# The scan's 3x3 convolution: the lower row's three taps on TensorE's 64-row tiles, the other six on VectorE alone

## The reference, cut to what matters

```python
xz = conv1x1(xin, in_proj_w)
xc, z = (xz[:, :Cm], xz[:, Cm:])                       # Cm = 64
z = jax.nn.silu(z)
xc = jax.lax.conv_general_dilated(xc, conv_w, (1, 1), 'SAME', feature_group_count=Cm, ...) + conv_b
xc = jax.nn.silu(xc)                                   # a 3x3 depthwise convolution of 64 channels
xh = xc.reshape(Bb, Cm, L)
xw = xc.transpose(0, 1, 3, 2).reshape(Bb, Cm, L)       # the same, column by column
```

## Time and profile before

| | |
|---|---|
| time, median of 3 runs | 3703.48 us (3699.1 to 3704.27) |
| the profiled execution: span | 3694.3 us |
| PE busy | 2966.0 us, 80% |
| PE weight loads busy | 1600.3 us, 43% |
| DVE busy | 2489.1 us, 67% |
| ACT busy | 2368.6 us, 64% |
| POOL busy | 1081.3 us, 29% |
| mean granted clock of TensorE | 0.93 |

### The profile page before, as it was taken

How to read it: one execution, slowest core, us unless ns; L and a number is a source line. 1 busy time by engine, 2 the same in 40 slices (tenths; PEclk the granted TensorE clock), 3 DMA queues, 4 the chain that set the end, 5 groups by cost and what they waited for, 6 DMA issues and landing times.

```text
span 3694.3 us, 53955 instructions
## 1 busy us (share of the span) xinstructions
PE 2966.0 (80%) x17500; PEld 1600.3 (43%) x17500; DVE 2489.1 (67%) x2565; ACT 2368.6 (64%) x2681; POOL 1081.3 (29%) x612
## 2 busy tenths in 40 slices
PE   3688876969978877787997887776998788768699
PEld 2344335435534434434553443443555344344355
DVE  5787656866478656687466964768636786577771
ACT  2887545468688745447778864543868877454484
POOL 0235103632034500463103530146210453025430
PEclk9899998979989999898998999888999999989899
DMA  2001473600200157440020034653002005555101
GB/s 67 17 1 39 119 203 104 164 9 0 69 27 1 44 133 215 112 125 9 0 90 5 0 91 120 198 142 79 9 9 86 0 0 141 130 173 146 40 0 52
DMA packets 137191, 274.31 MB, mean 74 GB/s; under 512 B 17139, under 2 KB 93622, under 8 KB 137014
## 3 DMA queue, kind: packets, MB, share of 16 engines
q1 hardware_dynamic: 137014, 272.01, 26.5%
HBM read 194.07 MB, written 77.88 MB: 74 GB/s over the span
## 4 chain that ended last, share of the span: by engine, by line
PE 50%; DVE 24%; issue 11%; ACT 9%; DMA 3%; POOL 1%; DVEq 1%; SPq 1%; ACTq 0%; POOLq 0%
PE psum L1074 31%; PE psum L1094 5%; PE psum L1327 5%; DVE work L1501 5%; DVE work L1473 3%; PE psum L1125 3%; DVE region L1602 3%; DVE psum L1492 2%; DVE region L277 2%; DVE work L1486 2%; DMA work<-scratch_dwc 2%; PE psum L1285 2%; PE psum L1286 1%; DVE region L1546 1%; DVE region L1670 1%
## 5 line engine op out<-in xcount | busy, mean ns | idle before, releaser
L1556 DVE SCALAR_TENSOR_TENSOR work<-region,cols,work 128x768 f32<-128x768 f32 x288 | 397.9, 1382 | 16.6 <-DVE work L1556 8.1
L735 POOL TENSOR_TENSOR region<-region 128x768 f32<-128x768 f32 x96 | 205.8, 2147 | 376.2 <-ACT region L919 370.5
L1074 PE MATMUL psum<-region,m_cen 128*128 128x384 f32 (+1 forms) x384 | 163.9, 553 | 171.0 <-DVE region L1670 64.0
L1074 PE MATMUL psum<-region,m_fc 128*128 128x384 f32 (+1 forms) x768 | 282.8, 491 | 11.0 <-ACT work L1026 11.0
L1327 PE MATMUL psum<-work,m_fc 128*128 128x384 f32 x768 | 282.7, 492 | 1.2 <-DVE region L1674 0.9
L699 POOL TENSOR_TENSOR work<-work 128x768 f32<-128x768 f32 x48 | 109.3, 2280 | 440.8 <-ACT work L840 370.9
L1074 PE MATMUL psum<-work,m_avg 128*128 128x384 f32 x576 | 225.6, 516 | 15.1 <-ACT work L881 7.2
L711 POOL TENSOR_TENSOR work<-work,region 128x768 f32<-128x768 f32 x96 | 174.5, 1818 | 214.1 <-DVE work L1486 214.1
L277 DVE SCALAR_TENSOR_TENSOR region<-region,cols 128x768 f32<-128x768 f32 x192 | 223.8, 1165 | 19.9 <-POOL region L735 9.9
L1026 ACT ACTIVATE work<-psum,cols 128x768 f32<-128x768 f32 x192 | 173.1, 901 | 91.1 <-PE psum L1074 89.2
L1473 DVE SCALAR_TENSOR_TENSOR work<-region,cols,work 128x768 f32<-128x768 f32 x144 | 192.6, 1358 | 52.4 <-POOL work L699 34.2
(11 more groups left out here) (234 smaller groups left out, 7539.0 us busy)
## 6 DMA issues: line engine op xcount, KB each, us to landing
work<-scratch_cpe SPq DMA_DIRECT2D x192, 196.0 KB, 4.1
work<-scratch_dwc SPq DMA_DIRECT2D x192, 196.0 KB, 4.1
work<-scratch_lepe SPq DMA_DIRECT2D x192, 196.0 KB, 3.9
region<-in_tab_ch SPq DMA_DIRECT2D x48, 768.0 KB, 5.3
region<-in_x SPq DMA_DIRECT2D x48, 384.0 KB, 3.3
region<-in_tab_tok SPq DMA_DIRECT2D x48, 384.0 KB, 3.2
out<-work SPq DMA_DIRECT2D x48, 384.0 KB, 2.4
scratch_cpe<-region SPq DMA_DIRECT2D x44, 392.0 KB, 4.4
```

What stands on the lines that cost most here:

```text
L735: g.tensor_tensor(chain_tile(conv, n, p), chain_tile(conv, n - 1, p), chain_tile(conv, n, p), ALU.add).then_inc(tap_done[n], 1)
L1074: last = pe.matmul(psum[:, bank + s, 0:HC], weights[:, :], moving(s), start=(n == 0), stop=(n == len(terms) - 1))
L1556: v.scalar_tensor_tensor(out=by_row(tile(acc + p)), in0=prow(k, b, *TAPS[n]), scalar=tap_weight(conv, TAPS[n]), in1=by_row(tile(acc + p)), ...
```

## The change: what it does

The taps of the row below go to TensorE, and ScalarE and GpSimd leave the convolution. `lower[n]` is `same_half` with its rows scaled by the tap of the row below at column offset `n - 1`; a late load puts these taps into the upper partitions of `cols` too. For each block TensorE does six matmuls on 64 rows of the array: for each of three column offsets, one on partitions 0 to 63 for the first four rows of the block (bank `2 * p`), one on partitions 64 to 127 for the last four (bank `2 * p + 1`). It does them before it waits for VectorE, and then two matmuls with `same_half` for the other six taps. VectorE does those six as three instructions: one product of a tensor and a column, and two that multiply and add.

`overlapped` gets a list of runs that are never folded into a loop; on TensorE the convolution's run is one, so that its twelve blocks are written out. SyncE waits for all loads to land before it issues the late loads. Two unused diagonal matrices and `dwl1` are no longer made; three matrices `lower` are.

```diff
-                if not all(1 <= b <= count - 2 for b in bs):
+                if n in static or not all(1 <= b <= count - 2 for b in bs):
                     return None
...
+        below = slice(at["l1taps"] + 3, at["l1taps"] + 6)
+        late_loads = [(cols[CM:P, below], t["cols"][0:CM, below])]
...
             sp.wait_ge(setup_vec, 1)
+            sp.wait_ge(setup_loaded, 16 * len(loads))
             for dst, src in late_loads:
...
-                    g.tensor_tensor(tile(4 + p), tile(p), tile(2 + p), ALU.add).then_inc(b_taps[0], 1)
...
-                    a.wait_ge(b_taps[0], done(i, b - 2))
-                    for n, signal_of in enumerate((b_first, b_second)):
-                        a.activation(by_row(tile(2 * n + p)), prow(3, b, *scan_tap(n)), ACT.Copy, scale=col("l1taps", n))\
-                            .then_inc(signal_of, 1)
-                return [(0, first_terms), (3, silu_u)]
+                return [(3, silu_u)]
...
                     pe.wait_ge(b_act, done(i, b - 2))
-                    pe.wait_ge(b_taps[3], done(i, b))
-                    product(2 * p, [(dwl1, image_rows(3, b, *scan_tap(5))), (same_half, static(tile(6 + p)))])\
-                        .then_inc(b_mm, 1)
+                    pe.wait_ge(a_act, done(i, following(b)))
+                    for n in range(3):
+                        for s in range(2):
+                            half = slice(CM * s, CM * s + CM)
+                            rows = padded(3)[half, ds(ROWS * b + (2 + (HALF - 1) * s), HALF), n:n + S]
+                            pe.matmul(psum[:, 2 * p + s, 0:HC], lower[n][half, :], rows, start=(n == 0), stop=False)
+                    pe.wait_ge(b_taps[2], done(i, b))
+                    for s in range(2):
+                        last = pe.matmul(psum[:, 2 * p + s, 0:HC], same_half[:, :], static(tile(6 + p))(s), start=False,
+                                         stop=True)
+                    last.then_inc(b_mm, 1)
...
+            v.wait_ge(late_loaded, 16 * len(late_loads))
+            for n in range(3):
+                v.tensor_scalar(lower[n][:, :], same_half[:, :], col("l1taps", 3 + n), None, ALU.mult)
...
+                def first_tap(b, p):
+                    if is_first(b):
+                        for q in range(2):
+                            v.wait_ge(h_store[q], i * (8 * NB) + 16)
+                    v.wait_ge(a_act, done(i, following(b)))
+                    v.tensor_scalar(by_row(tile(p)), prow(3, b, -1, -1), col("l1taps", 0), None, ALU.mult)\
+                        .then_inc(b_taps[0], 1)
+                def second_tap(b, p):
+                    v.wait_ge(b_taps[0], done(i, b))
+                    v.scalar_tensor_tensor(out=by_row(tile(4 + p)), in0=prow(3, b, -1, 0), scalar=col("l1taps", 1),
+                                           in1=by_row(tile(p)), op0=ALU.mult, op1=ALU.add).then_inc(b_taps[1], 1)
+                def third_tap(b, p):
+                    v.wait_ge(b_taps[1], done(i, b))
+                    v.wait_ge(b_mm, done(i, b - 2))
+                    v.scalar_tensor_tensor(out=by_row(tile(6 + p)), in0=prow(3, b, -1, 1), scalar=col("l1taps", 2),
+                                           in1=by_row(tile(4 + p)), op0=ALU.mult, op1=ALU.add).then_inc(b_taps[2], 1)
```

More of the change, by code:

```diff
@@ L98, in chained, with overlapped @@
             step(t)
-def overlapped(eng, count, runs):
+def overlapped(eng, count, runs, static=()):
     def blocks(t):
@@ L227, in build @@
         same_half = mat("same_half")
-        dwl1 = mat("dwl1")
+        lower = [mat(f"lower_{n}") for n in range(3)]
         w_dt = [mat(f"w_dt{n}") for n in range(2)]
@@ L234, in build @@
         convs = ("cpe1", "dwc", "lepe", "cpe2")
-        diag = {c: [mat(f"{c}_{n}") for n in range(9 - CHAIN)] for c in convs if c == "cpe2"}
         shifted = {c: mat(c + "_shifted", 3 * P) for c in convs[:3]}
@@ L306, in build @@
         a_act = signal("a_act", "a")
-        b_first = signal("b_first", "a")
-        b_second = signal("b_second", "a")
-        b_taps = [signal(f"b_taps{n}", "g" if n == 1 else "v") for n in range(1, 5)]
+        b_taps = [signal(f"b_taps{n}", "v") for n in range(3)]
         b_mm = signal("b_mm", "p")
@@ L460, in build @@
                               t["cols"].rearrange("(j c) n -> c j n", j=4)[:, :, c0:c0 + 3]))
-        late_loads = []
+        below = slice(at["l1taps"] + 3, at["l1taps"] + 6)
+        late_loads = [(cols[CM:P, below], t["cols"][0:CM, below])]
         for k in range(4):
@@ L471, in build @@
                                        t["x_proj"][2 * sweep + half, RANK + what:RANK + what + 1, :]))
-        def scan_tap(n):
-            return (-1, n - 1) if n < 3 else (1, n - 4)
         def by_row(ap):
@@ L693, in middle @@
                 clear_frame(padded(3), last=2)
[L695 to L698, removed]
-                    g.tensor_tensor(tile(4 + p), tile(p), tile(2 + p), ALU.add).then_inc(b_taps[0], 1)
-                pipelined(g, NB, [(1, first_sum)])
                 all_done(g, i - 1, h_mm)
@@ L1335, in middle @@
                        (3, g_variance), (4, up(3)), (4, down(2)), (2, g_centre)]
-                overlapped(pe, NB, [(0, mlp)] + following_runs)
-            overlapped(pe, NB, [(0, [(3, xz(0)), (0, l0(0))]), (NB, conv_run(0))])
+                overlapped(pe, NB, [(0, mlp)] + following_runs, static=(2,))
+            overlapped(pe, NB, [(0, [(3, xz(0)), (0, l0(0))]), (NB, conv_run(0))], static=(1,))
             with pe.Fori(0, B - 1, 1) as i:
@@ L1387, in _ @@
             link(v.reduce_sum(col("Dsum"), cols[:, at["l1_D"]:at["l1_D"] + 4], mybir.AxisListType.X))
[L1388 to L1392, removed]
             link(v.tensor_tensor(shift_mask[:, :], ident[:, 0:32], ident[:, 32:64], ALU.add))
@@ L1401, in _ @@
                                         None, ALU.mult)
-            v.tensor_scalar(dwl1[:, :], same_half[:, :], col("l1taps", 5), None, ALU.mult)
             v.tensor_scalar(w_in[:, :], raw_in, col("n1_g"), None, ALU.mult)
@@ L1465, in conv_run @@
             def conv_run(i):
[L1466 to L1478, removed]
+                def first_tap(b, p):
[14 more added lines that the diff above has]
+                                           in1=by_row(tile(4 + p)), op0=ALU.mult, op1=ALU.add).then_inc(b_taps[2], 1)
+                return [(2, first_tap), (2, second_tap), (2, third_tap)]
             def middle(i, following_runs):
```

## The result

The changed kernel takes 3672.22 us in the median (3667.39 to 3676.65), against 3703.88 for the kernel before on the same chip: a ratio of 0.9917, 95% interval 0.9901 to 0.9932, 31.7 us faster. Two later comparisons gave 0.9938 (0.9926 to 0.995) and 0.9907 (0.9886 to 0.9928), 21.5 and 33.6 us faster. The forecast was 3667 us. The profiled span fell from 3694.3 to 3665.6 us, by 28.7.

The account below looks back on a forecast made before the run. VectorE and GpSimd taking turns, 4.73 us a block, were taken as the bound; TensorE's 3.48 makes a stage 46.1 us, saving 36.5 together: 3694.3 - 36.5 = 3657.8, with 9.2 around it 3667 us, range 3650 to 3676.

Parts of the forecast that it names:

- VectorE and GpSimd as the bound before: Convolution stage before the change: VectorE's taps and GpSimd's sum take turns and bound a block at 4.73 us.
- VectorE's steps: VectorE per block after: a product of 0.72, two multiply-and-adds of 1.02, gaps of 0.45; 3.2 us, at most 3.9.
- TensorE's lower row, six waves: TensorE per block: twelve instructions on two 64x128 tiles, row halves side by side, in six waves, 2.10 us.
- TensorE's `same_half`, 1.38: TensorE per block: the product with `same_half` as four instructions of 0.32 plus 0.09 for the change of tiles, 1.38 us.
- The rule of the Trainium skill: TensorE: changing tiling mode drains it, two changes per block; priced from the trace at 0.09 and 0.16, within the 3.48.
- The stage: Convolution stage per image: 12 x 3.48 + 1.7 for the clock + 2.6 tail = 46.1 us, together saving 36.5.
- Clock: Start of the stage: one dip of 3.4 us at half speed, 1.7 lost; the later dips dropped.
- Head, set-up, written-out code: Stage head: nothing; set-up: nothing, at worst 2 us once; TensorE's written-out blocks: nothing taken, bound 12 us.
- the 9.2 us "around" the profiled span: Whole run: 9.2 us added to the forecast span of 3657.8, giving 3667 us.
- halves one after another: Rival, TensorE's lower row: row halves don't run side by side on 64x128 tiles, 14 us longer per image, 3759; 7%.
- A drain for a matmul's whole 0.48: Rival, TensorE: each change of tiles empties the array for 0.48, 4.2 a block, no change, 3701; 4%.
- Clock at the low level, VectorE or code in the way: Two rivals: clock stays at 0.50, 3827, 2%; VectorE or code fetch holds TensorE, half the gain lost, 3685, 12%.

Follow-up runs that it names:

- experiments 2 to 4: The changed kernel with ScalarE's two products and GpSimd's sum kept: 3694.11 us; then the sum on VectorE: 3693.04 us; or one product on VectorE, GpSimd summing: 3678.73 us.
- experiment 6: The changed kernel with a fourth VectorE instruction per block, a second copy of the first product into an unused tile: 3674.22 us, 0.9937 to the kernel before.
- experiment 1: The changed kernel with the lower row's six matmuls on all 128 rows, zero weights for the upper partitions: 3754.04 us, 1.014 to the kernel before.
- experiment 7: The changed kernel with the lower rows of two blocks, then both products, in eight PSUM banks: 3663.99 us, 0.989 to the kernel before.
- experiment 4: The changed kernel with GpSimd's sum kept, one of its two products on ScalarE, the other on VectorE: 3678.73 us, 0.9929 to the kernel before.

## Why the prediction was right, point by point

- **VectorE and GpSimd as the bound before**: right for the first bound, incomplete for the second. The working showed ScalarE busy for 44.7 of 52.5 us and passed over it; experiments 2 to 4 show that it would have been the next bound, 4.30 per block. The limits stand close together: 4.73 for VectorE with GpSimd, 4.30 for ScalarE, 3.62 for TensorE. The change takes work from ScalarE too, so the number did not suffer. ScalarE's figure stood in its timeline before the change: from the two products of one block to those of the next are 1062.84 - 1058.52 = 4.32 us, without idle time.

```profile
1058.52 1.76 ACT L840 ACTIVATE work<-region,cols 128x768 f32 x2
1060.31 0.90 ACT L829 ACTIVATE region<-psum,cols 64x768 f32 x1
1061.21 1.60 ACT L831 ACTIVATE region<-psum,cols 64x768 f32 x1
1062.84 1.76 ACT L840 ACTIVATE work<-region,cols 128x768 f32 x2
```

- **VectorE's steps**: the new product takes 0.61 (estimate 0.72), a block without waiting is 2.7 (3.62 less 0.91), below the 3.2. That TensorE doesn't wait for it is shown by experiment 6.
- **TensorE's lower row, six waves**: right in kind, 2.14 for 2.10. Pairs start 5 to 10 ns apart, and experiment 1 shows what the overlap is worth.
- **TensorE's `same_half`, 1.38**: this is the term that was mis-sized, with 1.49 measured. It was taken from the product at 650.32, which follows matmuls of its own height. The product that comes out of small tiles stands two rows below it: 1.56 from 653.80, against 1.45. Those 0.11 us are the second half of the price of a change, and they were in the rows. With the 0.04 of the lower row a block is 3.625: 48 x 0.145 = 7.0 us too little.
- **The rule of the Trainium skill ("TensorEngine Tiling (Array Packing)", Key Properties)**, that a change of the mode drains TensorE: the trace agrees in that a change costs 0.20 us, and experiment 7 confirms the price by taking half of the changes away. An emptied array the trace doesn't show: the first 128-row matmul starts at 1052.876, and the last 64-row one, from 1052.465, is given 0.481 us, so 0.07 us longer (ends of matmuls are modelled). No figure but the measured one entered.
- **The stage**: 12 x 3.625 + 1.7 + 2.6 = 47.8, which images 1 and 2 have. Images 0 and 3 meet the low clock for longer at the start (first block 6.2 us, 146.31 to 152.53, and 5.9, 2833.28 to 2839.17, not 5.3 as from 1041.84 to 1047.12). Together the stages save 28.1 instead of 36.5; of the 8.4 missing, 7.0 come from the block and 1.5 from these heads.
- **Clock**: right. One low stretch at the head and none later: behind the first block all of TensorE's blocks take 3.62 us, in all images of the three profiles. The 64-row tiles don't lower the clock.
- **Head, set-up, written-out code**: nothing was taken for them, and nothing is seen. The written-out blocks have no run of their own; TensorE shows no pause inside the stage. TensorE's set-up moved from 27.11 to 29.34 (29.2 was said), and L0 began at 56.5 us instead of 57.1. That image 0's stage began 4.0 us earlier (146.31, before 150.28) belongs to that one execution: in the two later profiles of the changed kernel it began at 150.0 and 149.9. Some 3.4 us the other way lie in the rest of the program (28.1 + 4.0 - 3.4 = 28.7, the fall of the span).
- **From span to median**: the 9.2 us "around" the profiled span were mostly not around it. A run's time is 1.8 to 2.0 us above its own span; the other 7.3 were that profiled run being faster than the median. After, the median is 6.6 above the span. So 3657.8 + 9.2 became 3665.6 + 6.6: the span 7.8 higher than said, and 2.6 of it given back by this. That the forecast came within 5 us is therefore partly luck: the saving was put at 36.5 us, the stages gave 28, and the three comparisons gave 31.7, 21.5 and 33.6.
- **The rivals**: halves one after another, refuted by the trace and priced by experiment 1 (3754, where 3759 was said). A drain for a matmul's whole 0.48: refuted, 0.20. Clock at the low level, VectorE or code in the way: none seen. The chances of the two slower rivals, 7% and 2%, add up to 0.09, where the summary of the chances has 0.08.

## What to carry to other kernels

Before work leaves the bounding pair of engines, write down the period of every engine in that stage: the second and third may stand 0.4 us below, and then only their removal together pays in full. When a price is read off a neighbouring row, take the row that stands behind the same kind of transition, since here the right figure was two lines further down. Interleave tile heights as rarely as the PSUM banks allow, keep the last group small for the sake of the tail, and look for a first block that can start during the pause.

## What the runs showed of the hardware that was not expected

- A change between 64x128 and 128x128 tiles costs 0.20 us at the full granted clock (2.4 GHz) with 384 float32 columns, half ahead of the first instruction and half behind it; the trace shows no weights loaded ahead across the change, as they are at every other step.
- GpSimd's sum and VectorE's multiply-and-add exclude each other almost wholly: 1.81 and 1.02 alone, and when they start within 0.06 us of each other, one keeps its length and the other ends up at 2.58 to 2.65 (experiment 4, image 1), against 2.83 for the two in a row. It is the one that starts later, except at 1074.88, where they start 0.01 us apart.
- Of one kernel, 14 runs spread from 3666 to 3684 us while the changed stage keeps its length to 0.5 us per image in three profiles. Span and mean granted clock go together over these runs (correlation -0.68); what sets the moments at which the clock changes level was not tried.
